# Softmax denominators in an attention kernel: sums of turned 32x32 blocks on VectorE in place of GpSimd's key sums and TensorE's transposes

## What is computed

```python
q, k, v = qkv[0], qkv[1], qkv[2]
sim = einsum('bhid,bhjd->bhij', q * SCALE, k)
sim = tanh(sim / SOFTCAP) * SOFTCAP
sim = where(causal_mask, -max, sim)
attn = softmax(sim, axis=-1)
out = einsum('bhij,bhjd->bhid', attn, v)
out = out * sigmoid(x @ w_gates)
out = out @ w_out
```

## Time and profile before

| | |
|---|---|
| median of three runs | 1632.26 us (1631.19 to 1633.91) |
| the profiled execution | 1630.03 us, span 1628.3 us |
| PE busy | 1599.3 us, 98% of the span |
| DVE busy | 902.9 us, 55% |
| POOL busy | 683.4 us, 42% |
| ACT busy | 584.5 us, 36% |
| attention stage | from about 35 to 1018 us |

### The profile page before, as it was taken

How to read it: one execution, slowest core, us unless ns; L and a number is a source line. 1 busy time by engine, 2 the same in 40 slices (tenths; PEclk the granted TensorE clock), 3 DMA queues, 4 the chain that set the end, 5 groups by cost and what they waited for, 6 DMA issues and landing times.

```text
span 1628.3 us, 24487 instructions
## 1 busy us (share of the span) xinstructions
PE 1599.3 (98%) x8384; PEld 1385.4 (85%) x8385; DVE 902.9 (55%) x1554; ACT 584.5 (36%) x996; POOL 683.4 (42%) x564
## 2 busy tenths in 40 slices
PE   7999999999999999999999999999999999999996
PEld 6888888888888888888888888787999988999995
DVE  4777656677656677665665667433662393222221
ACT  4444443443434334434344344333111222333332
POOL 4676654556446456454465554201210003333342
PEclk9999999999999999999999999999999999999999
DMA  8776454576676776675686777553431016777753
GB/s 293 281 285 226 173 203 161 214 280 257 245 260 221 255 293 239 242 283 209 238 301 240 280 288 272 204 190 97 148 148 42 1 46 209 234 237 245 233 91 44
DMA packets 83345, 342.24 MB, mean 210 GB/s; under 512 B 8560, under 2 KB 8560, under 8 KB 77744
## 3 DMA queue, kind: packets, MB, share of 16 engines
q1 hardware_dynamic: 70224, 303.18, 50.9%
q0 software_dynamic: 13024, 37.79, 9.8%
HBM read 220.89 MB, written 120.05 MB: 209 GB/s over the span
## 4 chain that ended last, share of the span: by engine, by line
PE 87%; DVE 4%; DMA 4%; issue 2%; POOL 2%; ACT 0%; POOLq 0%; SPq 0%; DVEq 0%; ACTq 0%
PE bank L357 27%; PE bank L359 27%; PE bank L358 27%; DMA out<-x_early,ids_e 2%; PE bank L1712 2%; PE bank L1843 1%; PE bank L1951 1%; DMA pre_raw<-pre 1%; PE bank L1811 0%; POOL pre_split L595 0%; PE bank L1850 0%; DVE resid L1198 0%; PE bank L1625 0%; DMA rows<-x_rows,ids_e 0%; DVE stats L1037 0%
## 5 line engine op out<-in xcount | busy, mean ns | idle before, releaser
L636 POOL TENSOR_TENSOR probs<-probs,causal 128x256 f32<-128x256 f32 x126 | 91.0, 743 | 404.2 <-ACT probs L827 404.2
L359 PE MATMUL bank<-store,wqk 128*128 128x512 f32 x512 | 202.2, 395 | 0.0
L358 PE MATMUL bank<-store,wqk 128*128 128x512 f32 x512 | 201.9, 394 | 0.0
L357 PE MATMUL bank<-store,wqk 128*128 128x512 f32 x512 | 201.8, 394 | 0.0
L1198 DVE SCALAR_TENSOR_TENSOR resid<-bank,factor,resid 128x512 f32<-128x512 f32 x256 | 188.7, 739 | 2.6 <-PE bank L359 2.5
L1192 DVE TENSOR_TENSOR q_lo<-bank,q_hi 128x512 fp32r<-128x512 f32 x64 | 44.2, 691 | 192.1 <-ACT q_hi L873 192.1
L825 ACT ACTIVATE probs<-bank 128x512 f32<-128x512 f32 x189 | 85.9, 529 | 156.1 <-PE bank L359 156.1
L1206 DVE TENSOR_TENSOR p_lo<-probs,p_hi 128x1280 fp32r<-128x1280 f32 x63 | 120.6, 1914 | 2.2
L595 POOL TENSOR_TENSOR pre_split<-pre_raw,pre_split 128x1528 fp32r<-128x1528 f32 x34 | 120.1, 3532 | 0.1
L744 POOL DMA_INDIRECT out<-x_early,ids_e x39 | 61.6, 1580 | 138.3 <-DMA out<-x_early,ids_e 103.2
L359 PEld LDWEIGHTS bank<-store,wqk 128*128 128x128 f32 x512 | 96.1, 188 | 22.8
(11 more groups left out here) (333 smaller groups left out, 4165.9 us busy)
## 6 DMA issues: line engine op xcount, KB each, us to landing
pre_parts<-pre_split SPq DMA_DIRECT2D x34, 1528.0 KB, 7.0
wqk<-wqk_parts SPq DMA_DIRECT2D x96, 512.0 KB
pre_raw<-pre SPq DMA_DIRECT2D x34, 764.0 KB, 7.7
store<-wv_parts SPq DMA_DIRECT2D x12, 2048.0 KB, 9.4
wo<-wo_parts SPq DMA_DIRECT2D x48, 512.0 KB, 8.1
expert_w<-pre_parts SPq DMA_DIRECT2D x8, 2816.0 KB
wqk_parts<-wqk SPq DMA_DIRECT2D x16, 1024.0 KB, 5.2
expert_w<-pre_parts SPq DMA_DIRECT2D x8, 1536.0 KB
```

The lines of the kernel that those rows point to most:

```text
L357: nc.tensor.matmul(out_ap, a_hi, b_hi, start=first, stop=False)
L358: nc.tensor.matmul(out_ap, a_hi, b_lo, start=False, stop=False)
L359: return nc.tensor.matmul(out_ap, a_lo, b_hi, start=False, stop=last)
L636: nc.gpsimd.tensor_tensor(diagonal, diagonal, causal[:, :, :], ALU.mult).then_inc(S["masked"], 1)
```

## The change

`sum_probs` on PE, `sum_keys` on POOL and the tile `key_sums` go. DVE has a new `sum_keys(u - 1)` behind y_add 2 (and gate_add), ahead of the statistics and o_low: four reductions over the columns of `probs`, in which each 32x32 block is turned, so that the sum runs over 32 keys. They leave for each query 4 key tiles in each of four groups of 32 partitions. `y_factors` copies the groups of partitions 1 to 3 beside group 0, sums the 16 numbers of each query into bank 6, multiplies each group of queries by its part of the gate's denominator and takes the reciprocal. ACT waits for `keys_summed` in place of the two waits before. All four V splits of a group are on POOL, and those waiting for them count so.

```diff
-            def sum_keys(u, masked=None):
-                pool.wait_ge(S["masked"], masked or 2 * u + 2)
-                if u:
-                    pool.wait_ge(S["sum_ready"], u)
-                nc.gpsimd.tensor_tensor(key_sums[:, P:], probs[:, P:SEQ], probs[:, POFF[1]:POFF[1] + SEQ - P], ALU.add).then_inc(S["sums_step"], 1)
-                pool.wait_ge(S["sums_step"], 2 * u + 1)
-                nc.gpsimd.tensor_tensor(key_sums[:, 2 * P:], key_sums[:, 2 * P:], probs[:, POFF[2]:POFF[2] + 2 * P], ALU.add).then_inc(S["sums_step"], 1)
-                pool.wait_ge(S["sums_step"], 2 * u + 2)
-                nc.gpsimd.tensor_tensor(key_sums[:, 3 * P:], key_sums[:, 3 * P:], probs[:, POFF[3]:POFF[3] + P], ALU.add).then_inc(S["sums_done"], 1)
...
                 if u:
                     mask(u - 1)
-                if u:
-                    sum_keys(u - 1)
...
                 if u % TB == 0 and u // TB + 1 < GROUPS:
-                    low_v(u // TB + 1, 0)
-                    low_v(u // TB + 1, 1)
+                    for k in range(KC):
+                        low_v(u // TB + 1, k)
...
             def softmax_part(u):
                 if u:
 
                     act.wait_ge(S["p_lo_done"], u)
-                    act.wait_ge(S["sums_done"], u)
-                    act.wait_ge(S["sum_ready"], u)
+                    act.wait_ge(S["keys_summed"], u)
...
+            def sum_keys(u):
+
+                if u == 0:
+                    dve.wait_ge(S["sums_zeroed"], 1)
+                for j in range(TB):
+                    cols = probs[:, POFF[j]:POFF[j] + SEQ - P * j].rearrange("p (c k) -> p c k", k=BLOCK)
+                    last = nc.vector.tensor_reduce(sums[:, j * P // BLOCK:, 0, j], cols, mybir.AxisListType.X, ALU.add, apply_transpose=True)
+                last.then_inc(S["keys_summed"], 1)
+
             def y_factors(u):
 
-
                 b, h = divmod(u, HEADS)
-                dve.wait_ge(S["sum_ready"], u + 1)
-                nc.vector.tensor_reduce(denom[:, 0, :], bank[6][:, :].rearrange("p (t k) -> p t k", t=TB), mybir.AxisListType.X, ALU.add).then_inc(S["den_summed"], 1)
-                dve.wait_ge(S["den_summed"], u + 1)
-                link(nc.vector.tensor_tensor(denom[:, 1, :], denom[:, 0, :], gate_den[:, TB * b:TB * b + TB, h], ALU.mult))
-                nc.vector.reciprocal(factor[:, u % 2, :], denom[:, 1, :]).then_inc(S["factor_done"], 1)
+                dve.wait_ge(S["keys_summed"], u + 1)
+                for a in range(1, P // BLOCK):
+                    last = nc.vector.tensor_copy(sums[0:BLOCK, :, a, :], sums[a * BLOCK:a * BLOCK + BLOCK, :, 0, :])
+                link(last)
+                of = bank[6][0:BLOCK, 0:SEQ // BLOCK]
+                link(nc.vector.tensor_reduce(of, sums[0:BLOCK, :, :, :].rearrange("p c a j -> p c (a j)"), mybir.AxisListType.X, ALU.add))
+                for a in range(P // BLOCK):
+                    rows_of = slice(a * BLOCK, a * BLOCK + BLOCK)
+                    last = nc.vector.tensor_tensor(denom[rows_of, :], of.rearrange("p (t a) -> p t a", a=P // BLOCK)[:, :, a], gate_den[rows_of, TB * b:TB * b + TB, h], ALU.mult)
+                link(last)
+                nc.vector.reciprocal(factor[:, u % 2, :], denom[:, :]).then_inc(S["factor_done"], 1)
...
                 if gates_slot(u):
                     gate_add(gates_slot(u))
+                if u:
+                    sum_keys(u - 1)
...
-                g = u // TB + 1
-                if u % TB == 0 and g < GROUPS:
-                    for k in range(KC // 2, KC):
-                        low_v(g, k)
...
-            def sum_probs(u):
-
-                pe.wait_ge(S["sums_done"], u + 1)
-                if u:
-                    pe.wait_ge(S["den_summed"], u)
-                for i in range(TB):
-                    of = key_sums if i else probs
-                    last = nc.tensor.transpose(bank[6][:, i * P:i * P + P], of[:, i * P:i * P + P], ident[:, :])
-                last.then_inc(S["sum_ready"], 1)
...
                 if u:
                     values(u - 1)
-                    sum_probs(u - 1)
```

More of the change, by code:

```diff
@@ L21 @@
 PCOLS = sum(SEQ - P * j for j in range(TB))
+BLOCK = 32
 POFF = {0: 0, 1: SEQ, 3: 2 * SEQ - P, 2: 2 * SEQ}
@@ L203, in build @@
         gate_den = sb("gate_den", [P, TILES, HEADS])
-        denom = sb("denom", [P, 2, TB])
+        denom = sb("denom", [P, TB])
         factor = sb("factor", [P, 2, TB])
-        key_sums = sb("key_sums", [P, SEQ])
+        sums = sb("sums", [P, SEQ // BLOCK, P // BLOCK, TB])
         wqk = sb("wqk", [P, 2, 2, KC, DH], F32R)
@@ L255, in build @@
         pre_loaded pre_hi pre_lo pre_stored
-        q_ready k_ready vt_ready s_ready pv_ready sum_ready y_ready
+        q_ready k_ready vt_ready s_ready pv_ready y_ready
         qk_hi_done v_hi_done o_hi_done tanh_done exp_done
-        q_lo_done k_lo_done v_lo_done p_lo_done o_lo_done den_summed factor_done y_added masked sums_step sums_done stored
+        q_lo_done k_lo_done v_lo_done p_lo_done o_lo_done sums_zeroed keys_summed factor_done y_added masked stored
         ids_loaded zeros_ready zero_filled_x spare_filled step prefix_ready prefix_read prefix_e_read chosen_ready route_x_done route_e_done
@@ L272, in build @@
         ZTILES = 4
-        BLOCK = 32
         NCH = {"x": KC, "s": SC, "e": IC}
@@ L468, in _ @@
                 if u % TB == 1 and g < GROUPS:
-                    sp.wait_ge(S["wv_split"], KC // 2 * (g + 1) + 1)
-                    sp.wait_ge(S["wv_split_dve"], KC // 2 * (g + 1) - 1)
+                    sp.wait_ge(S["wv_split"], KC * (g + 1) - 1)
                     store_wv(g)
@@ L683, in _ @@
             nc.gpsimd.tensor_tensor(probs[:, 0:P], probs[:, 0:P], causal[:, 0, :], ALU.mult).then_inc(S["masked"], 1)
-            sum_keys(last, 2 * last + 4)
             rsqrt(ln)
@@ L1256, in low_v @@
                 nc.vector.tensor_tensor(wv_lo[:, k, :], wv_raw[:, k, :], wv_hi[:, k, :].bitcast(F32), ALU.subtract).then_inc(S["wv_split_dve"], 1)
+            nc.vector.memset(sums[:, :, 0, :], 0.0).then_inc(S["sums_zeroed"], 1)
             first_stats(0)
@@ L1418, in _ @@
                 y_add(U - 2, i, TAIL_BANKS[0][i])
+            sum_keys(U - 1)
             y_factors(U - 1)
@@ L1680, in weights_ready @@
                     if v < GROUPS:
-                        pe.wait_ge(S["wv_split"], KC // 2 * (v + 1) + 1)
-                        pe.wait_ge(S["wv_split_dve"], KC // 2 * (v + 1) - 1)
+                        pe.wait_ge(S["wv_split"], KC * (v + 1) - 1)
                     else:
@@ L1873, in _ @@
             transpose_rows("x", 0, 1)
-            sum_probs(U - 1)
             for i in range(TB):
```

## The result

The changed kernel takes 1699.26 us (median; 1698.90 to 1702.86), the kernel before, on the same chip, 1632.92. The ratio is 1.0412, 95% interval 1.0394 to 1.0430: slower, by the forecast mechanism and about 20 us above the forecast number. The profiled execution took 1699.28 us with a span of 1697.5, where before's took 1630.03 with 1628.3: 69.2 us more span, with the sum of the prediction at 48.

A forecast was written before the change was run, and what follows sets the result against it. PE, busy 98% of the span, was taken as the bound. Terms: -30 us for removed transposes, +66 for the split colliding with p_lo, +12 for a late DVE, sum +48, so 1680 us (own range 1655 to 1708; wider 1635 to 1712).

The forecast's parts named there:

- PE 30.1 us shorter: On PE, four transposes per unit go between values and the next product: 0.47 us per unit, 30.1 over 64.
- Rival 4: On PE, nothing like the forecast happens because the transposes were hidden; called excluded, within 0.2% given 0.03.
- DVE's own durations: On DVE, four turning reductions take 1.8 us and the factors about 1.55 where 1.0 stood: 2.3 more per unit.
- Rival 2: On DVE, turning reductions run at half rate or less: 1724 us, or over 1900 at 7.2 us; chance 0.09.
- the period of 14.9 us in units 9 to 16: Sign that the forecast is right: in the attention stage, units 9 to 16 each take 14.9 us.
- The collision, 66 us: POOL's earlier low_pre holds up DVE's p_lo, so PE waits before output product 2: 2.1 us in 25 of 34 units.
- Rival 1: In units with low_pre, the split does not hold DVE's p_lo, so the kernel is faster: 1617 us; chance 0.16.
- rival 3: Only the 12 units whose ACT high part is on time now collide, the other loads staying late: 1642 us; chance 0.08.
- the step that followed the split's store to the next load: An earlier low_pre lets the next pre_raw load start earlier, 4.5 us more before it is due: all 34 units collide.
- Nothing for the V splits: Four V splits on POOL, none on DVE, ahead of a mask that is not late: nothing, to 1 us either way.
- the paragraph on the later split: On low_pre from unit 18: a running DVE or POOL operation with operands in SBUF holds the other engine.
- 12 us for a late DVE: DVE's added work delays y_add 3 beside statistics or routing: 0.5 to 1.5 us in some 14 units, between 3 and 25.

The follow-up runs named there:

- experiment 1: The changed kernel, with POOL's split of the later weights (low_pre) waiting until DVE's p_lo is done; 1635.88 us, ratio 1.0002.
- experiment 2: The kernel before, with only POOL's split of the later weights (low_pre) moved ahead of the key sums; 1715.72 us, ratio 1.0481.
- experiment 5: The kernel before, with only one part of the change: all four V splits on POOL; 1638.97 us, ratio 1.0028.
- experiment 4: The changed kernel, with low_pre waiting for p_lo and two of the four V splits back on DVE; 1626.13 us, ratio 0.9955.
- experiment 6: The changed kernel, with low_pre waiting for p_lo and y_add 3 ahead of the factors, routing and normalized rows; 1614.64 us, ratio 0.9877.
- experiment 3: The changed kernel, with each low_pre split made as two instructions of 764 columns and no new wait; 1640.85 us, ratio 1.0042.
- experiment 10: The changed kernel, with low_pre waiting for p_lo, y_add 3 ahead of the factors, two V splits back on DVE; 1612.27 us, ratio 0.9872.

## Why the prediction was right, and where its sum was not

**PE 30.1 us shorter.** Nearly: 0.42 us per iteration and 26.5 over the 63 that can be read, 3 us less than the step. It put 0.23 between the first two matmuls of the product; the rows show 678.75 to 679.04, 0.29. Rival 4 falls: the transposes were not hidden.

**DVE's own durations.** Right: the reductions 1.68 (1.8 said), the factors 1.8 (1.55 said). Rival 2 falls. One sign was read too widely: the period of 14.9 us in units 9 to 16 holds from 14 on, since iterations 10 and 11 have four transposes (15.34 us, 15.77 before) and 12 the gate matmuls (17.18), and 9 is one of the late ones.

**The collision, 66 us.** Right in its order, its two ends and its size, and shown from two sides: taken out of the changed kernel (experiment 1) and put into the kernel before (experiment 2), 2.13 us each time in a plain iteration (2.1 said). With gate matmuls ahead of the product it is 0.3 (17.50 for 17.18), with four transposes 1.7 (17.05 for 15.35), in the last one 2.96 (15.14 for 12.18). Over 34: 25 x 2.13 + 6 x 1.7 + 2 x 0.3 + 2.96 = 67.0. Two of these iterations show `p_hi` at 3.4 us instead and `p_lo` at 1.49, POOL having come first: the same end, as said. Rival 1 falls. So does rival 3: ACT's waits for `pre_raw` are gone, as said, and POOL's split waits for ACT in all 34, never longer than 1.3 us. With the split late again (experiment 1) the loads are late again. POOL's and ACT's waits of the changed kernel, then of experiment 1:

```profile
POOL pre_split L593 <- ACT pre_split L773: 19.4, 34, 1.3
```

```profile
ACT pre_split L774 <- DMA pre_raw<-pre: 25.5, 21, 3.1
```

So the step that followed the split's store to the next load, and counted 34 collisions instead of 12, was right.

**Nothing for the V splits.** Wrong: "nothing, to 1 us either way" costs about 5 us alone (experiment 5) and 10 with the new copies (experiments 1 and 4). The step called the mask behind the splits not late, and in iteration 1 it is, which costs 1.9 us. And it did not ask which DVE operations run beside the splits, although the paragraph on the later split used that mechanism.

**12 us for a late DVE.** Near in its number, by luck. Of the 20.2 us of new losses in iterations 0 to 17, about 10 go with the V splits, as these iterations hold the same work as those of experiment 1; about 10 are left for this term, for 12 said.

But they are not where it said. The step spread it over some 14 units with statistics or routing. Most of them lie behind iteration 18, and they do cost what it said when nothing covers them: in experiment 1 iterations 19, 20, 22, 23, 35, 36, 38, 39, 51 and 52 lose 0.6 to 1.5 us each, 10.3 in all. In the changed kernel the stalls for the split cover all of it but 0.33 us in iterations 22 and 38 each, while the first rival took only 3 us as covered. In their place the first ones cost more: 1.2 and 1.0 in 3 and 4, behind the routing, 2.2 in 5 beside the 4.2 of the V splits, with a fall of the clock, 3.2 in 6, behind statistics and routing together, and 1.1 in 7.

With the collision away (experiment 1) lateness costs 31.9 us in all, the 10 of the V splits included: 26.5 gained, and the attention 5.4 longer (1002.84 - 997.40). Moving `y_add` 3 takes back 23.7 us of the attention (14.8 in iterations 0 to 17, 8.9 behind), sharing the V splits 10.2, partly the same. The copies, at 4.6 and 5.4 times their length in iterations 4 and 8, stand in one stretch with everything else between o_low and `y_add` 3.

**The granted clock.** Not in the sum at all. In seven places in the attention PE falls to half speed during or shortly behind a wait for `y_add`. One of these waits ends at 523.26:

```profile
523.00:525.00 2.00, 1.74 (x5) 0.64 1.02 394
525.00:527.00 2.00, 2.00 (x8) 0.50 0.98 284
527.00:529.00 2.00, 2.00 (x13) 1.00 0.56 232
...
542.00:544.00 2.00, 2.00 (x10) 1.00 1.05 361
```

(windows of the changed kernel: start and end, length, PE busy and matmuls, granted clock, DMA share, GB/s). Iterations 30, 34, 46, 54 and 58 have such a fall and take 18.61 to 18.68 us instead of 17.06: 1.6 us each, 8 in all. The other two are in iterations 5 and 9 and part of the 20.2.

The ledger of the attention: -26.5 + 67.0 + 8.0 + 20.2 = 68.7, where 67.8 was measured. The 0.9 between them is in four iterations: the kernel before is slow in 55 (16.21 us for 15.35) and in 61 (13.29, 12.17 in the changed kernel), which is 1.6 us of gain beyond the 0.42 each, and 22 and 38 lose the 0.33 each. From the sum's 48 to 68.7 it is 20.7: 10.2 for the V splits, 8.0 for the clock, 3.5 for the smaller gain, 1.0 for the collision, and 2.0 less for a late DVE. The span grew by 1.4 us more outside these iterations, which was not traced. So the forecast was right in its main term, 66 of 67, and short by the V splits and the clock, which it had at nothing.

## What to carry to other kernels

Taking short operations off an engine also moves up what was queued behind them: look at what long instruction now starts, and beside which operations of the other engine, since either can hold the other. An instruction whose result the bottleneck engine waits for belongs ahead of work that is wanted an iteration later; this was worth nothing before the change and 21 us behind the change with its late split. A change that takes 26 us of work off TensorE came out as a loss of 66, and as a gain of 20 once two orders were mended (experiment 6).

## What the runs showed of the hardware

- **Who is next.** With DVE and POOL both asking for the memory, the engine that did not have it goes next, in every row shown here: a split that was issued 0.15 us into `p_hi` ran ahead of a `p_lo` that came at its end, and in experiment 3 halves and `p_lo` alternate.
- **Small copies.** A copy of 64 columns on 32 partitions takes 183 ns, and up to 1251 when GpSimd's splits run beside it, in the changed kernel:

```profile
L1220 DVE COPY sums<-sums x192: 182/183/1251, 50.3 to 1085.7; 32x64 f32<-32x64 f32 x192
```

- **The clock after a wait.** Waits of the same length end differently. At 523.26 and at 541.90 PE had waited 1.87 us for the same line, with the same work around it; behind the first the granted clock was 0.50 (1.2 GHz) for some 3 us, behind the second it stayed at 1.00 (2.4 GHz). Experiment 1 has three such falls in the attention, experiments 4, 6 and 10 one each, the kernel before none. What decides it was not tried.
